# A gated cross-attention and MoE-attention layer: the cross-attention runs two slots sooner, the second normalised x is transposed by VectorE blocks and DRAM

## The chip, the cores and the metric

The kernel runs on one core of one Trainium2 chip. The metric is the device time of one execution in microseconds (us), lower is better. The kernel before took 817.31 us (median of 3 runs, 815.43 to 818.0).

## The reference

The input x has 64 sequences of 128 tokens and 128 channels, and each sequence has a context of 77 rows. Everything is float32.

```python
# cross-attention, gated
xn = layernorm(x)                       # over channels, no scale
keys, values = ctx @ Wk.T, ctx @ Wv.T ; queries = xn @ Wq.T
x  = x + tanh(g_xattn) * softmax(queries @ keys.T / sqrt(128)) @ values
# mixture-of-experts attention, gated
h  = layernorm(x)                       # 16 experts
logits = normalise(h) @ normalise_columns(sim_matrix) - sigmoid(gates)
w  = softmax over the experts with logits > 0 (the two largest if there is none) of relu(logits)
q, k, v = sum_e w[:, e] * (h @ q_proj[e]), the same with k_proj, v_proj
o  = softmax(q @ k.T / sqrt(128)) @ v   # within a sequence
x  = x + tanh(g_ffn) * sum_e w[:, e] * (o @ o_proj[e])
```

## The kernel before, in words

The 64 sequences are worked in 16 groups of 4 (`G = 4`, `NG = 16`), so that a tile has 512 token columns. Each engine has its instruction stream written out by hand in the same frame: `passes(body)` calls `body(i)` for i = 0 to 17, and a body runs over 16 slots `s`, one for each expert. In pass i, TensorE accumulates q, k and v of group i (line 1292: in each slot 9 matmuls of 128x512 in fp16, for high and low halves of weights and of scaled tokens), and between the experts it does work of other groups: the cross-attention of group g1 = i + 2, the second layer norm and the gate of g2 = i + 1, the attention and the output experts of gc = i - 1, and the end of the output experts of gd = i - 2. The output experts are 8 pairs a group (`y_pair`, two times three matmuls each, line 1321), one in every second slot.

Nothing but the semaphores orders the engines against each other. Each engine takes its own stream in order, so a wait on one instruction holds everything behind it on that engine. SyncE (its DMA queue is SPq in the rows) issues nearly all DMAs, and also waits in order.

Steps that the change touches, in the kernel before, with slot numbers:

- Cross-attention of g1: `ctxT_out` (ScalarE, slot 6), `kx_product` (TensorE, 7), `kxT_out` (ScalarE, 7), the scores (`small_product`, four parts within expert 9, line 1385), `x_max` (VectorE, 9, line 1125), `x_exps` and `vx_out` (ScalarE, 10, lines 784 and 792), `vx_product` (TensorE, 10, line 1431), the 32x32 block transpose of px (VectorE, 11), its way through DRAM (SyncE, 12: `px_rows` out, wait, `px_mix` in), `pxT_out` (ScalarE, 12, line 806), `att_product` (TensorE, 14, line 1445), `x1_add` (VectorE, 14, line 1136), `second_stats` (VectorE, 15, lines 923 and 927).
- Second norm of g2, in the following pass: `second_rstd` (GpSimd, 0, lines 594 to 599), `second_norm` (GpSimd, 1), `x2_norm` (ScalarE, 1, line 725), `x2_transpose` (TensorE, 2, line 1401: four 128x128 transposes into bank m0), `x2T_out` (ScalarE, 2, line 733), then the gate logits (`small_product` in expert 4, line 1377), `gate_logits`, `gate_mask`, `gate_softmax` (VectorE, 4, 5 and 6), and `weight_rows` with three `spread_q` broadcasts of 512 KB (SyncE, 9).
- `x2T_p` then holds the transposed tokens, and `zq_scale` (VectorE, line 1063), `zq_high` (ScalarE, 690) and `zq_low` (GpSimd, 611) make each expert's scaled tokens `LEAD = 4` slots ahead of their matmuls.
- In slot 15 ScalarE empties the q, k and v banks (line 845); TensorE's next pass waits for that.
- In slot 7 TensorE makes oT of gc, ScalarE copies its high half and VectorE makes the low half (`oT_low`, line 1078); the third matmul of the first `y_pair` in slot 8 waits for the low half.

v, the first normalised x (from group 3 on) and the attention weights pc already take a way through DRAM in place of a TensorE transpose: VectorE transposes 32x32 blocks (line 994), `blocks_out` writes 256 KB to `blk_rows` (line 428), and `blocks_in` reads it back with four DMAs of 64 KB in block order (line 434).

Of the kernel before, what the change touches and what calls it, by code (L numbers as in the profile page):

```python
# [13 lines left out]
P = 128  # L14
# [16 lines left out]
X_HEAD = 3  # L31

# [17 lines left out]
def flamingo_gated_moe_attention(nc, x, ctx_in, g_xattn, g_ffn, Wk, Wq, Wv, sim_matrix, gates,  # L50
# [11 lines left out]
    with ExitStack() as ctx:  # L62
# [97 lines left out]
        blk_rows = nc.dram_tensor("blk_rows", [3, 4, 32, N], F32, kind="Internal").ap()  # L160
# [4 lines left out]
        pc_blk = sb("pc_blk", [P, 4, G, 32])  # L165
        w_rows = nc.dram_tensor("w_rows", [NG, E * G, P], F32, kind="Internal").ap()
# [83 lines left out]
        x2T_sb = sem("x2T_sb")  # L250
        x2T_moved = sem("x2T_moved")
# [132 lines left out]

        def before(g, e, slots):
            return (g, e - slots) if e >= slots else (g - 1, E + e - slots)
# [8 lines left out]
        MAX_AT, SHARE_AT = (0, 2), ((0, 4), (0, 6))  # L395
# [4 lines left out]
        def _(sp):  # L400
# [83 lines left out]

            def body(i):
                g1, g2, gc, gd = i + 2, i + 1, i - 1, i - 2
                for s in range(E):
                    if s in (2, 4):
                        spread_q(i, PAIRS - 2 + s // 4)
                    if s == 2 and 0 <= gc < NG - 1:  # L490
                        wait(sp, v_blk_done, gc + 1)
                        wait(sp, v_mix_in, 64 * gc)
                        blocks_out(0, v_blk, v_blk_out)
                    if s == 2 and X_HEAD <= g1 < NG:
                        wait(sp, xn_blk_done, g1 - X_HEAD + 1)
                        wait(sp, xn_mix_in, 64 * (g1 - X_HEAD))
                        blocks_out(1, xn_blk, xn_blk_out)
# [25 lines left out]
                    if s == 11 and has(gd) and gd < NG - 1:  # L523
                        store(gd)
                    if s == 12 and has(g1):
                        n = g1 - P_HEAD
                        wait(sp, px_blk_done, n + 1)
                        wait(sp, px_mix_in, 48 * n)
                        sp.dma_start(px_rows.rearrange("i t r -> (i t) r"),
                                     px_blk[:].rearrange("p j b n -> p (j b n)")).then_inc(px_blk_out, 16)  # L530
                        wait(sp, px_blk_out, 16 * (n + 1))
                        wait(sp, pxT_sb, g1)
                        for j in range(3):
                            keys = min(32, S - 32 * j)
                            sp.dma_start(px_mix[32 * j:32 * j + keys].rearrange("t i b n -> t i (b n)"),
                                         px_rows[:, 0:keys, P * j:P * (j + 1)].rearrange("i t r -> t i r")
                                         ).then_inc(px_mix_in, 16)
# [24 lines left out]
        def _(pool):  # L562
# [102 lines left out]
        def _(act):  # L665
# [55 lines left out]
            def x2_norm(g):  # L721
                wait(act, rstd2_step, 3 * g + 3)
                wait(act, x2T_ps, g)
# [113 lines left out]
            def body(i):  # L837
                g1, g2, gc, gd = i + 2, i + 1, i - 1, i - 2
                for s in range(E):
                    if s == E - 1 and has(i):  # L840
# [6 lines left out]
                    if s == 6 and has(g1):  # L847
                        ctxT_out(g1)
# [13 lines left out]
                    if s == 1 and has(g2):  # L862
                        x2_norm(g2)
                    if s == 2 and has(g2):
# [21 lines left out]
                    if s == 5 and has(g1):  # L886
                        xnT_out(g1)
                    if s == 5 and has(g2):
                        gate_exps(g2)
                    if s == 7 and has(g1):  # L890
# [5 lines left out]
                    if s == 10 and has(g1):  # L896
                        x_exps(g1)
                    if s == 10 and has(g1):
# [3 lines left out]
                    if s == 12 and has(g1):  # L902
# [17 lines left out]
        def _(dve):  # L920
# [257 lines left out]
            def body(i):  # L1178
                g1, g2, gc, gd = i + 2, i + 1, i - 1, i - 2
                for s in range(E):  # L1180
                    for g, e in zq_at(i, s):
                        zq_scale(g, e)
                    if s == 11 and has(g1):
# [33 lines left out]
                    if s == 3 and has(g2):  # L1217
                        x2_norm_inverse(g2)
                    if s == 4 and has(g2):
                        gate_logits(g2)  # L1220
                    if s == 5 and has(g2):
                        gate_mask(g2)
                    if s == 6 and has(g2):
                        gate_softmax(g2)
                    if s == 9 and has(g1):
# [3 lines left out]
                    if s == 11 and has(g1):  # L1229
# [5 lines left out]
                    if s == 14 and has(g1):  # L1235
                        x1_add(g1)
                    if s == 15 and has(g1):
                        second_stats(g1)
                    if (i, s) == MAX_AT:
# [23 lines left out]
        def _(pe):  # L1263
# [108 lines left out]
            def small_product(i, s, b):  # L1372
                g1, g2 = i + 2, i + 1
                if s == 4 and has(g2):
                    if b == 0:
                        wait(pe, x2T_sb, g2 + 1)
                    last = nc.tensor.matmul(m0[:, b * E:(b + 1) * E], x2T[:, tok(b)], sn[:],  # L1377
# [3 lines left out]
                if s == 9 and has(g1):  # L1381
# [67 lines left out]
            def head():  # L1449
# [7 lines left out]
                for b in range(G):  # L1457
                    small_product(-2, 9, b)
# [13 lines left out]
                for b in range(G):  # L1472
                    small_product(-1, 9, b)
# [4 lines left out]
            def body(i):  # L1478
                g1, g2, gc, gd = i + 2, i + 1, i - 1, i - 2
                for s in range(E):  # L1480
# [17 lines left out]
                    if s == 2 and has(g2):  # L1498
# [6 lines left out]
                    if s == 5 and g1 < X_HEAD:  # L1505
# [3 lines left out]
                    if s == 7 and has(g1):  # L1509
# [21 lines left out]
                    if s == 10 and has(g1):  # L1531
                        vx_product(g1)
                    if s == 14 and has(g1):
# [33 lines left out]
```

## Time and profile before

| | |
|---|---|
| median of 3 runs | 817.31 us |
| the profiled execution | 816.46 us |
| its span, first to last instruction | 814.6 us |
| busy: TensorE, VectorE, GpSimd, ScalarE | 96%, 74%, 59%, 53% |
| DMA, mean of 16 engines | 45.7% for the queue of SyncE |
| granted TensorE clock, mean | 1.000 |

The profiled execution is 1.86 us longer than its span; that part lies around the first and the last instruction. The stretches of one pass below are cut at the start of the attention scores (line 1394). In a row of the timeline the first number is when an instruction started, the second how long it took; matmuls overlap, so the distance between two starts says what one costs TensorE, and not its duration. "idle before" is time in which an engine waited, and the name behind the arrow is what ended it.

### The profile page before, as it was taken

Reading aid. Unit: us, or ns where it says so; the run is one execution under the profiler, and the core shown is the slowest. Engines: PE = TensorE matmul, PEld = TensorE weight load, DVE = VectorE, ACT = ScalarE, POOL = GpSimd, SP = SyncE. Lnnn points to the kernel's source line nnn. Section 1 sums busy time; section 2 is a strip of 40 time slices with the busy share of each in tenths; the row PEclk is TensorE's granted clock in tenths of the full one; section 3 lists DMA queues with packets and bytes.
Section 4 is the critical chain, followed back from the end, with each engine's and each line's share of the span. In section 5 each row is a group of like instructions: output and inputs, shape, how many; then the busy total and the mean of one; then the engine's idle time right before and its main releaser. Section 6 shows DMA issues by size and latency. Waiting matters only on the chain.

```text
span 814.6 us, 13947 instructions
## 1 busy us (share of the span) xinstructions
PE 784.9 (96%) x4011; PEld 421.3 (52%) x4011; DVE 602.7 (74%) x2026; ACT 434.5 (53%) x1130; POOL 483.4 (59%) x703
## 2 busy tenths in 40 slices
PE   5589999999999999999999999999999999999998
PEld 4445554555555555555555555555555555544444
DVE  2878686869598686868868686886868687685648
ACT  5555645456464645646464564646456454643435
POOL 3275656565585656567665656766565675655534
PEclk9999999999999999999999999999999999999999
DMA  7464664544544443455444445545444554343200
GB/s 184 123 217 151 187 195 138 179 159 139 170 153 148 144 163 118 139 172 155 147 144 135 145 137 171 158 146 144 150 129 138 169 165 136 112 138 119 64 14 27
DMA packets 89195, 116.50 MB, mean 143 GB/s; under 512 B 13734, under 2 KB 62398, under 8 KB 89118
## 3 DMA queue, kind: packets, MB, share of 16 engines
q1 hardware_dynamic: 88398, 115.52, 45.7%
q8 instruction: 32, 0.52, 0.2%
q14 instruction: 45, 0.37, 0.1%
q10 hardware_dynamic: 720, 0.08, 0.1%
HBM read 94.27 MB, written 21.30 MB: 142 GB/s over the span
## 4 chain that ended last, share of the span: by engine, by line
PE 71%; DVE 15%; DMA 5%; issue 3%; POOL 2%; ACT 2%; SPq 2%; DVEq 0%; ACTq 0%; POOLq 0%
PE acc_q L1292 15%; PE acc_k L1292 15%; PE acc_v L1292 15%; PE oT_p L1321 8%; PE y L1321 8%; DVE x_all L1093 3%; DVE zq_full L1063 3%; PE m L1394 2%; PE m L1445 1%; DVE logit L1008 1%; DMA px_rows<-px_blk 1%; PE m L1431 1%; PE m L1385 1%; PE m L1377 1%; DMA stage<-in_L_ffn_k_proj_dram 1%
## 5 line engine op out<-in xcount | busy, mean ns | idle before, releaser
L611 POOL TENSOR_TENSOR zq<-zq_full,zq 128x512 f16<-128x512 f32 x256 | 297.9, 1171 | 278.0 <-ACT zq L690 277.1
L690 ACT ACTIVATE zq<-zq_full 128x512 f16<-128x512 f32 x256 | 159.7, 633 | 219.6 <-DVE zq_full L1063 219.2
L1292 PE MATMUL acc_q<-zq,w_hi 128*128 128x512 f16 x510 | 193.3, 379 | 0.0
L1292 PE MATMUL acc_k<-zq,w_hi 128*128 128x512 f16 x510 | 193.3, 379 | 0.0
L1292 PE MATMUL acc_v<-zq,w_hi 128*128 128x512 f16 x510 | 193.2, 379 | 0.0
L1063 DVE TENSOR_TENSOR zq_full<-wq_bc,x2T_p 128x512 f32<-128x512 f32 x256 | 167.6, 668 | 2.7 <-DMA wq_bc<-w_rows 2.3
L1093 DVE SCALAR_TENSOR_TENSOR x_all<-y,w_out,x_all 128x128 f32<-128x128 f32 x356 | 121.9, 342 | 60.1 <-issue 40.7
L1093 DVE SCALAR_TENSOR_TENSOR x_all<-oT_p,w_out,x_all 128x128 f32<-128x128 f32 x356 | 121.4, 341 | 0.1
L626 POOL TENSOR_TENSOR x_all<-stage,x_all 128x128 f32<-128x128 f32 x240 | 100.4, 456 | 19.9 <-DVE x_all L1093 13.4
L1292 PE MATMUL acc_q<-zq,w_lo 128*128 128x512 f16 x255 | 96.7, 379 | 0.0
L1292 PE MATMUL acc_v<-zq,w_lo 128*128 128x512 f16 x255 | 96.6, 379 | 0.0
L1292 PE MATMUL acc_k<-zq,w_lo 128*128 128x512 f16 x255 | 96.6, 379 | 0.0
L1321 PE MATMUL y<-w_hi,oT 128*128 128x512 f16 x236 | 89.6, 380 | 1.8 <-ACT stage L717 0.9
L1321 PE MATMUL oT_p<-w_hi,oT 128*128 128x512 f16 x236 | 89.5, 379 | 0.0
L1292 PEld LDWEIGHTS acc_v<-zq,w_hi 128*128 128x128 f16 x510 | 53.6, 105 | 53.3
L1292 PEld LDWEIGHTS acc_q<-zq,w_hi 128*128 128x128 f16 x510 | 51.8, 102 | 51.4 <-POOL zq L611 0.6
L1292 PEld LDWEIGHTS acc_k<-zq,w_hi 128*128 128x128 f16 x510 | 49.8, 98 | 53.3
L1136 DVE SCALAR_TENSOR_TENSOR x_all<-m,rsum_x,x_all 128x128 f32<-128x128 f32 x64 | 18.0, 344 | 74.2 <-PE m L1445 74.2
L717 ACT ACTIVATE stage<-oT_p,w_out 128x128 f32<-128x128 f32 x116 | 32.6, 361 | 30.6 <-issue 19.2
L1321 PE MATMUL oT_p<-w_lo,oT 128*128 128x512 f16 x118 | 44.7, 379 | 0.0
L1321 PE MATMUL y<-w_lo,oT 128*128 128x512 f16 x118 | 44.7, 379 | 0.0
L1292 PEld LDWEIGHTS acc_k<-zq,w_lo 128*128 128x128 f16 x255 | 26.8, 105 | 26.7
(223 smaller groups left out, 1108.3 us busy)
## 6 DMA issues: line engine op xcount, KB each, us to landing
wq_bc<-w_rows SPq DMA_DIRECT2D x128, 512.0 KB, 4.3
blk_rows<-v_blk SPq DMA_DIRECT2D x15, 256.0 KB, 4.2
v_mix<-blk_rows SPq DMA_DIRECT2D x60, 64.0 KB, 2.0
blk_rows<-pc_blk SPq DMA_DIRECT2D x15, 256.0 KB, 3.2
pcT<-blk_rows SPq DMA_DIRECT2D x60, 64.0 KB, 2.0
out_dram<-x_all SPq DMA_DIRECT2D x15, 256.0 KB, 4.0
blk_rows<-xn_blk SPq DMA_DIRECT2D x13, 256.0 KB, 2.6
xn_mix<-blk_rows SPq DMA_DIRECT2D x52, 64.0 KB, 3.4
```

Source lines behind the costliest of these rows:

```text
L611: nc.gpsimd.tensor_tensor(zq[:, 1, e % Z_SLOTS, :], zq_full[:, e % F_SLOTS, :], zq[:, 0, e % Z_SLOTS, :], ALU.subtract).then_inc(zq_lo_poo ...
L626: nc.gpsimd.tensor_tensor(total, y_sc[:, n // 2 % 2, b, j, :], total, ALU.add).then_inc(y_pool_added, 1)
L690: nc.scalar.activation(zq[:, 0, e % Z_SLOTS, :], zq_full[:, e % F_SLOTS, :], ACT.Copy).then_inc(zq_hi_done, 1)
L717: last = nc.scalar.activation(dst, bank[:, tok(j)], ACT.Copy, scale=w_out[:, g % 2, e, b0 + b:b0 + b + 1])
L1008: link(nc.vector.tensor_tensor(logit[:], logit[:], sig[:].unsqueeze(1).broadcast_to([P, G, E]), ALU.subtract), 1)
L1063: nc.vector.tensor_tensor(zq_full[:, e % F_SLOTS, :], wq_bc[:, e // 2 % W_SLOTS, e % 2], x2T_p[:], ALU.mult).then_inc(zq_full_done, 1)
L1093: nc.vector.scalar_tensor_tensor(out=rows(x_all, g, b0 + b), in0=bank[:, tok(j)], scalar=w_out[:, g % 2, e, b0 + b:b0 + b + 1], in1=rows(x ...
L1136: last = nc.vector.scalar_tensor_tensor(out=rows(x_all, g, b), in0=m1[:, tok(b)], scalar=rsum_x[:, b:b + 1], in1=rows(x_all, g, b), op0=AL ...
L1292: last = nc.tensor.matmul(acc[m][:], w[:, m, s, :], zq[:, half, s % Z_SLOTS, :], start=(s == 0 and n == 0), stop=(s == E - 1 and n == 2))
L1321: last = nc.tensor.matmul(bank[:], oT[:, g % 2, half, tok(b)], w[:, O, QUAD * k:QUAD * (k + 1), :].rearrange("p e c -> p (e c)"), start=(n ...
L1377: last = nc.tensor.matmul(m0[:, b * E:(b + 1) * E], x2T[:, tok(b)], sn[:], start=True, stop=True)
L1394: done = nc.tensor.matmul(m1[:, tok(b)], qT[:, tok(b)], kT[:, tok(b)], start=True, stop=True)
```

## The change

Cross-attention of g1 moves two slots forward in every pass but pass 0 (`sooner(i)` is 2 there, and 0 in pass 0), and `second_stats`, `second_rstd`, `second_norm` and `x2_norm` of g1 now come in the same pass, in slots 13, 13, 15 and 15. From group 3 on (`X2_HEAD = 3`) the second normalised x takes the way through DRAM in place of `x2_transpose`. In pass 0 the gate steps move one slot back (`late(i)` is 1 there), the second part of the share of the largest output weight moves from slot 6 to slot 7, `xn_transpose` and `xnT_out` from 5 to 6, and px goes out in slot 11, ahead of a broadcast. SyncE's order changes: `weight_rows` in slot 8, px out and in interleaved with the broadcasts in slots 9 and 10, first normalised x back in slot 3, and the new transfers in slots 0 and 1.

```diff
+        blk_rows = nc.dram_tensor("blk_rows", [4, 4, 32, N], F32, kind="Internal").ap()
+        x2_blk = sb("x2_blk", [P, 4, G, 32])
+        x2_mix = sb("x2_mix", [P, 4, G, 32])
...
+        def sooner(i):
+            return 0 if i == 0 else 2
+        def late(i):
+            return 1 if i == 0 else 0
-        MAX_AT, SHARE_AT = (0, 2), ((0, 4), (0, 6))
+        MAX_AT, SHARE_AT = (0, 2), ((0, 4), (0, 7))
...
 # SyncE, body
-                    if s in (2, 4):
-                        spread_q(i, PAIRS - 2 + s // 4)
-                    if s == 2 and 0 <= gc < NG - 1:
+                    if s == 0 and X2_HEAD <= g2 < NG:
+                        wait(sp, x2_blk_done, g2 - X2_HEAD + 1)
+                        wait(sp, x2_mix_in, 64 * (g2 - X2_HEAD))
+                        blocks_out(3, x2_blk, x2_blk_out)
+                    if s == 0 and 0 <= gc < NG - 1:
                         wait(sp, v_blk_done, gc + 1)
                         wait(sp, v_mix_in, 64 * gc)
                         blocks_out(0, v_blk, v_blk_out)
+                    if s == 1 and X2_HEAD <= g2 < NG:
+                        wait(sp, x2_blk_out, 16 * (g2 - X2_HEAD + 1))
+                        wait(sp, x2T_sb, g2)
+                        blocks_in(3, x2_mix, x2_mix_in)
+                    if s in (2, 4):
+                        spread_q(i, PAIRS - 2 + s // 4)
...
-                    if s == 4 and X_HEAD <= g1 < NG:
+                    if s == 3 and X_HEAD <= g1 < NG:
                         wait(sp, xn_blk_out, 16 * (g1 - X_HEAD + 1))
...
-                    if s == 9 and has(g2):
+                    if s == 8 and has(g2):
                         weight_rows(g2)
-                        for j in range(3):
+                    if s == 9 and has(g1) and i > 0:
+                        px_out(g1)
+                    if s == 9:
+                        spread_q(g2, 0)
+                    if s == 10 and has(g1) and i > 0:
+                        px_in(g1)
+                    if s == 10:
+                        for j in (1, 2):
                             spread_q(g2, j)
+                    if s == 11 and has(gd) and gd < NG - 1:
+                        store(gd)
+                    if s == 11 and i == 0:
+                        px_out(g1)
+                        px_in(g1)
...
 # GpSimd, body
-                    if s == 0 and i > 0 and has(g2):
+                    if s == 0 and i == 1:
                         second_rstd(g2)
+                    if s == 13 and i > 0 and has(g1):
+                        second_rstd(g1)
                     for g, e in zq_at(i, s):
                         zq_low(g, e)
-                    if s == 1 and has(g2):
+                    if s == 1 and i < 2:
                         second_norm(g2)
+                    if s == 15 and i > 0 and has(g1):
+                        second_norm(g1)
...
 # ScalarE
             def x2T_out(g):
-                wait(act, x2T_ps, g + 1)
                 wait(act, x2T_moved, g)
                 wait(act, logit_ps, g)
-                nc.scalar.activation(x2T[:], m0[:], ACT.Copy, scale=X_UP).then_inc(x2T_sb, 1)
+                if g < X2_HEAD:
+                    wait(act, x2T_ps, g + 1)
+                    nc.scalar.activation(x2T[:], m0[:], ACT.Copy, scale=X_UP).then_inc(x2T_sb, 1)
+                else:
+                    wait(act, x2_mix_in, 64 * (g - X2_HEAD + 1))
+                    nc.scalar.activation(x2T[:].rearrange("p (b i n) -> p b i n", b=G, n=32),
+                                         x2_mix[:].rearrange("p i b n -> p b i n"), ACT.Copy,
+                                         scale=X_UP).then_inc(x2T_sb, 1)
...
+                    if s == E - 1 and i > 0 and has(g1):
+                        x2_norm(g1)
                     if s == E - 1 and has(i):
                         wait(act, cscore_ps, i)
...
+                    if s == 3 and i > 1 and has(g2):
+                        x2T_out(g2)
...
 # VectorE, body (px blocks, x_max, x_sum, x1_add: slot - sooner(i); gate: slot + late(i))
+                    if s == 13 and i > 0 and has(g1):
+                        second_stats(g1)
...
+                    if s == 15 and i > 0 and has(g1):
+                        wait(dve, x2_done, g1 + 1)
+                        wait(dve, x2_blk_out, 16 * (g1 - X2_HEAD))
+                        blocks_transposed(x2_blk, x2[:], x2_blk_done)
...
 # TensorE, body (kx_product, scores, vx_product, att_product: slot - sooner(i))
-                    if s == 2 and has(g2):
+                    if s == 2 + late(i) and g2 < X2_HEAD:
                         x2_transpose(g2)
-                    if s == 5 and g1 < X_HEAD:
+                    if s == 6 and g1 < X_HEAD:
                         xn_transpose(g1)
```

## Rows read from the trace of the kernel before

**Rows 1.** The page, busy time by engine: us, share of the span, instructions.
```profile
PE 784.9 (96%) x4011; PEld 421.3 (52%) x4011; DVE 602.7 (74%) x2026; ACT 434.5 (53%) x1130; POOL 483.4 (59%) x703
```

**Rows 2.** Stretches of one pass: us, busy PE, PEld, DVE, ACT, POOL, clock, DMA share, GB/s.
```profile
184.84:232.08 47.24, 47.24 (x249) 25.35 (x248) 36.91 (x127) 26.13 (x69) 29.52 (x43) 1.00 0.48 149
...
326.55:373.99 47.44, 47.38 (x249) 25.36 (x248) 36.74 (x127) 26.07 (x70) 29.96 (x44) 1.00 0.48 149
```

**Rows 3.** TensorE's waits over the span: us in total, times, longest.
```profile
PE m L1401 <- ACT x L725: 3.0, 2, 1.8
...
PE oT_p L1283 <- DVE wmax_d L961: 1.2, 1, 1.2
PE oT_p L1522 <- DMA pcT<-blk_rows: 1.1, 1, 1.1
...
PE y L1321 <- ACT stage L717: 0.9, 1, 0.9
...
PE m L1445 <- ACT pxT L806: 0.8, 1, 0.8
```

**Rows 4.** Timeline of TensorE in one steady pass.
```profile
424.11 0.60 PE L1401 MATMUL m<-ident,x 128*128 128x128 f32 x4
424.55 0.38 PE L1321 MATMUL y<-w_hi,oT 128*128 128x512 f16 x1
...
428.22 0.29 PE L1377 MATMUL m<-sn,x2T 128*128 128x16 f32 x2
...
442.26 0.38 PE L1321 MATMUL y<-w_lo,oT 128*128 128x512 f16 x1
442.70 0.39 PE L1321 MATMUL y<-w_hi,oT 128*128 128x512 f16 x1
...
444.01 0.34 PE L1385 MATMUL m<-kxT,xnT 128*128 128x77 f32 x2
444.19 0.38 PE L1292 MATMUL acc_q<-zq,w_hi 128*128 128x512 f16 x1
...
459.41 1.06 PE L1445 MATMUL m<-vx,pxT 77*128 77x128 f32 x8
460.30 0.38 PE L1321 MATMUL y<-w_hi,oT 128*128 128x512 f16 x1
```

**Rows 5.** Timeline of VectorE, the same pass.
```profile
430.58 1.19 DVE L1008 TENSOR_TENSOR logit<-logit,sig 128x64 f32<-128x64 f32 x1
...
441.95 0.69 DVE L1078 TENSOR_TENSOR oT<-oT_p,oT 128x512 f16<-128x512 f32 x1 [1.18 <-ACT oT L895]
...
446.22 0.48 DVE L1125 TENSOR_REDUCE nmax_x<-m 128x4 f32<-128x308 f32 x1 [0.21 <-PE m L1385]
...
460.50 1.13 DVE L1136 SCALAR_TENSOR_TENSOR x_all<-m,rsum_x,x_all 128x128 f32<-128x128 f32 x4 [5.29 <-PE m L1445]
...
465.10 0.38 DVE L927 BATCH_NORM_AGGREGATE mv<-bn 128x2 f32<-128x6 f32 x4
...
465.97 0.70 DVE L994 STREAM_TRANSPOSE v_blk<-vT 128x512 f32<-128x512 f32 x1
```

**Rows 6.** Timeline of ScalarE, the same pass.
```profile
456.27 0.63 ACT L806 ACTIVATE pxT<-px_mix 77x512 f32<-77x512 f32 x1 [2.19 <-DMA px_mix<-px_rows]
...
462.53 0.60 ACT L845 ACTIVATE qT<-acc_q 128x512 f32<-128x512 f32 x1 [2.56 <-PE acc_q L1292]
...
468.68 1.64 ACT L725 ACTIVATE x<-x_all,shift,rstd 128x128 f32<-128x128 f32 x4
```

**Rows 7.** Timeline of GpSimd, the root for the second norm, first and last step.
```profile
466.30 0.23 POOL L594 TENSOR_SCALAR shift<-mv 128x4 f32<-128x4 f32 x1
...
468.02 0.20 POOL L599 TENSOR_TENSOR shift<-shift,rstd 128x4 f32<-128x4 f32 x1
```

**Rows 8.** Issue to landing, by tile: v_blk (its 15 writes).
```profile
DMA to landing us min/median/max: 4.1/4.2/4.8
```

**Rows 9.** The same for the DRAM tensor blk_rows (mostly its 172 reads).
```profile
DMA to landing us min/median/max: 1.8/2.1/4.8
```

More of the change, by code:

```diff
@@ L483, in head, with px_out, px_in @@
                     spread_q(0, j)
+            def px_out(g):
+                n = g - P_HEAD
+                wait(sp, px_blk_done, n + 1)
+                wait(sp, px_mix_in, 48 * n)
+                sp.dma_start(px_rows.rearrange("i t r -> (i t) r"),
+                             px_blk[:].rearrange("p j b n -> p (j b n)")).then_inc(px_blk_out, 16)
+            def px_in(g):
+                n = g - P_HEAD
+                wait(sp, px_blk_out, 16 * (n + 1))
+                wait(sp, pxT_sb, g)
+                for j in range(3):
+                    keys = min(32, S - 32 * j)
+                    sp.dma_start(px_mix[32 * j:32 * j + keys].rearrange("t i b n -> t i (b n)"),
+                                 px_rows[:, 0:keys, P * j:P * (j + 1)].rearrange("i t r -> t i r")
+                                 ).then_inc(px_mix_in, 16)
             def body(i):
@@ L846, in body @@
                                                  scale=1.0 / (X_UP * W_UP)).then_inc(acc_sb[m], 1)
-                    if s == 6 and has(g1):
+                    if s == 6 - sooner(i) and has(g1):
                         ctxT_out(g1)
@@ L861, in body @@
                                              ACT.Copy).then_inc(v_tok_sb, 1)
-                    if s == 1 and has(g2):
+                    if s == 1 and i < 2:
                         x2_norm(g2)
-                    if s == 2 and has(g2):
+                    if s == 2 + late(i) and i < 2:
                         x2T_out(g2)
@@ L885, in body @@
                                              ACT.Copy).then_inc(cpT_sb, 1)
-                    if s == 5 and has(g1):
+                    if s == 3 and i > 1 and has(g2):
+                        x2T_out(g2)
+                    if s == (5 if i else 6) and has(g1):
                         xnT_out(g1)
-                    if s == 5 and has(g2):
+                    if s == 5 + late(i) and has(g2):
                         gate_exps(g2)
-                    if s == 7 and has(g1):
+                    if s == 7 - sooner(i) and has(g1):
                         kxT_out(g1)
@@ L895, in body @@
                         nc.scalar.activation(oT[:, gc % 2, 0, :], oT_p[:], ACT.Copy).then_inc(oT_hi_done, 1)
-                    if s == 10 and has(g1):
+                    if s == 10 - sooner(i) and has(g1):
                         x_exps(g1)
-                    if s == 10 and has(g1):
                         vx_out(g1)
@@ L901, in body @@
                         x2T_move(g2)
-                    if s == 12 and has(g1):
+                    if s == (11 if i else 12) and has(g1):
                         pxT_out(g1)
@@ L1182, in body @@
                         zq_scale(g, e)
-                    if s == 11 and has(g1):
+                    if s == 11 - sooner(i) and has(g1):
                         wait(dve, xexp_done, g1 + 1)
@@ L1216, in body @@
                         blocks_transposed(pc_blk, pc[:], pc_blk_done)
-                    if s == 3 and has(g2):
+                    if s == 3 + late(i) and has(g2):
                         x2_norm_inverse(g2)
-                    if s == 4 and has(g2):
+                    if s == 4 + late(i) and has(g2):
                         gate_logits(g2)
-                    if s == 5 and has(g2):
+                    if s == 5 + late(i) and has(g2):
                         gate_mask(g2)
-                    if s == 6 and has(g2):
+                    if s == 6 + late(i) and has(g2):
                         gate_softmax(g2)
-                    if s == 9 and has(g1):
+                    if s == 9 - sooner(i) and has(g1):
                         x_max(g1)
@@ L1228, in body @@
                         first_stats(g1 + 1)
-                    if s == 11 and has(g1):
+                    if s == 11 - sooner(i) and has(g1):
                         x_sum(g1)
@@ L1373, in small_product @@
                 g1, g2 = i + 2, i + 1
-                if s == 4 and has(g2):
+                if s == 4 + late(i) and has(g2):
                     if b == 0:
                         wait(pe, x2T_sb, g2 + 1)
+                        wait(pe, vx_sb, g2 + 1)
                     last = nc.tensor.matmul(m0[:, b * E:(b + 1) * E], x2T[:, tok(b)], sn[:],
@@ L1380, in small_product @@
                         last.then_inc(logit_ps, 1)
-                if s == 9 and has(g1):
+                if s == 9 - sooner(i) and has(g1):
                     if b == 0:
@@ L1508, in body @@
                         ctx_transpose(g1)
-                    if s == 7 and has(g1):
+                    if s == 7 - sooner(i) and has(g1):
                         kx_product(g1)
@@ L1530, in body @@
                         y_end_sums()
-                    if s == 10 and has(g1):
+                    if s == 10 - sooner(i) and has(g1):
                         vx_product(g1)
-                    if s == 14 and has(g1):
+                    if s == 14 - sooner(i) and has(g1):
                         att_product(g1)
```

34 lines of the change are left out of this document (12 added, 22 removed).

## The prediction

> **What bounds the kernel now.** I read the busy table first: TensorE is busy 96% of the span, VectorE 74%, the others under 60% [rows 1]. Then I cut the span into passes at the attention scores. In four passes (137 to 327 us) TensorE is busy for the whole 47.24 us; in the eight from 327 to 706 us a pass takes 47.44 us and about 0.06 us of it shows as idle [rows 2]. The granted clock is 1.00 throughout, the upper level of 2.4 GHz, so no clock enters the sum. A steady pass is a full TensorE queue: what leaves that queue is gained one for one, and other engines matter only if they come late. The extra 0.2 us has a place in the timeline: the third matmul of the first output pair starts 0.44 us after the second, not 0.22 (442.26 to 442.70), and VectorE's oT_low runs from 441.95 to 442.64 just before it [rows 4, 5]. VectorE worked from the gate logits until there almost without a gap, and one of its steps, the subtraction of the sigmoid, took 1.19 us [rows 5]. Last, TensorE's waits outside the steady passes: 1.8 us for x2, 1.2 us for the maximum of the output weights and 0.8 us for pxT in pass 0, 1.1 us for pcT and 0.9 us for a staged pair in pass 1 [rows 3].
>
> **The transposes that leave TensorE.** The four transposes take TensorE's queue from 424.11 to 424.55, that is 0.44 us [rows 4]. Groups 3 to 15 lose them: 13 x 0.44 = 5.7 us. Each of them lies in a pass with a full queue, so the whole sum is on the path. One page speaks of another size: the Trainium skill, TensorE: Matmul & The Clock Gate, section Part 4: PE-mode transpose, gives about 275 ns for one 128x128 transpose in a kernel's context; 52 of them would be 14.3 us by that. The recorded durations here are near that figure, but the starts in the full queue are 0.11 us apart, and the sum goes by the starts.
>
> **What comes in their place, and what hides it.** VectorE gets one block transpose a pass, 0.70 us by the one for v [rows 5], on an engine with over 9 us idle in a pass [rows 2]. ScalarE's copy of x2T stays. SyncE gets one write of 256 KB and four reads of 64 KB. None is on TensorE, so each costs nothing while its result is in time. I follow the chain in the clock of the pass shown, before any of the gain is taken off.
>
> The attention product starts at 459.41; two slots sooner means ahead of two experts (18 matmuls at 0.216 us) and one pair (6 more), 5.2 us, so 454.2, done 455.1 [rows 4]. Then: x1_add 0.2 us later, 1.1 us; one zq_scale 0.6; statistics 1.3 (0.9 for the four, 0.4 for the aggregates, of which the row is shown); bn2 is ready near 458.3 [rows 5]. GpSimd's root runs 1.92 us (466.30 to 468.22) [rows 7], and it stands ahead of a low half now: done 460.2. The low halves behind it slide 2 us, but they are made 5 us or more ahead of their matmuls. x2_norm takes 1.64 us [rows 6]: done near 462.0. It stands ahead of the emptying of q, k and v, which begins at 462.53 [rows 6]. Cover 0.5 us, and some 0.5 us more before the next pass's matmuls would stand. After its cover each us is one us a pass.
>
> VectorE's block transpose comes behind the adds of the pair of slot 14. That pair begins on TensorE at 460.30 [rows 4], ends 1.3 us on, and its eight adds take 2.1 us, so the blocks are ready at about 464.6. SyncE issues the write at 464.9; a write of this size lands 4.2 us after issue [rows 8]: 469.1. Four reads are issued in 1.7 us and land 2.1 us after issue by the median [rows 9], near 472.5. ScalarE is busy with the exponentials until about 473.0, so x2T is ready at 473.6. TensorE asks for it in expert 4 of the next pass, 428.22 plus one new period of 46.8: 475.0 [rows 4]. Cover 1.4 us. The operation is not in the trace of before for this tile, so its bounds: with every read at the 1.8 us minimum the answer is the same, since ScalarE is then the later one; with the write at 4.8 us (the slowest of v) and the reads at 4.8 us [rows 8, 9] x2T comes 2.8 us later than I reckon, and TensorE would stand 1.4 us a pass, 18 us in all. I take the median, since the slow ones lie in the first passes beside the input loads. Behind the new wait on SyncE stand v's transfer, two broadcasts, xn and pc. v's blocks are ready only after x2's. The broadcast for experts 12 and 13 is issued 4 us later than before but used in slot 8; xn's reads end near slot 5; pc goes out within 0.4 us of its old time, because its blocks are what it waits for.
>
> **The cross-attention two slots sooner.** Scores and product both move over two experts and a pair, so px keeps its time for the way through DRAM: pxT is done at 456.9 for a product at 459.41 [rows 4, 6], a cover of 2.5 us; because oT's product is no longer between them I reckon 1.8 us. No broadcast stands ahead of px out any more, one stands ahead of px in; I count these against each other. What changes for TensorE is where its own fillers lie: the scores, 4 x 0.18 us (444.01 to 444.19 for one) [rows 4], and the value product (0.87 us) now come between the gate logits and the first output pair. That gives VectorE's gate chain 1.6 us more, and it takes on x_max there, 0.4 us between starts [rows 5], and must wait for the scores. By my count oT_low ends 0.4 us ahead of its matmul, where now it is 0.2 us late. So the 0.2 us goes: 8 passes x 0.2, and 0.3 us in pass 14, 1.9 us. Bounds: 1.9 us gained, or with a second step as slow as the 1.19 us one, 1 us more on VectorE and 0.6 us lost a pass.
>
> That step is a place for a rule. It took 1.19 us in the slow passes for a tile that others of its size take in 0.23, and it ended with GpSimd's low half beside it. The Trainium skill, SBUF — State Buffer, section SBUF: two separate sides, says that VectorE with two SBUF inputs and GpSimd take one port pair in turn, each for a whole instruction. By that rule the root and the low halves that move could block another step of the chain; the row can't tell which, and it stands in the rival below with bounds of its own from rows.
>
> **The first passes.** In pass 0 the transpose comes a slot later, so x2 is there, but TensorE then comes to experts whose low halves GpSimd has only just made; the wait for the maximum goes as well; and px of group 2 may then be later than its product, since its write stands behind three broadcasts. Bounds 0 and 3.8 us, the sum of the three waits [rows 3]; I take 1.5, under the middle, since each of them has a follower. In pass 1 the scores come ahead of oT's product (0.7 us of 1.1 [rows 3]), v is written ahead of a broadcast, and ScalarE no longer waits for pxT ahead of the staged pair: bounds 0 and 2.0 us, I take 2.0, since both mechanisms are direct.
>
> **Sum.** 5.7 + 1.9 + 1.5 + 2.0 = 11.1 us. The profiled execution took 816.46 us, which is 0.85 us under the median of the runs. 816.46 - 11.1 = 805.4, and put against the median 806.2. I predict 806.2 us.
>
> **Rivals.**
> 1. Only the transposes pay. The early waits turn into others (broadcasts, low halves, DMAs beside the loads) and VectorE's chain keeps its 0.2 us: 5.7 us, 817.3 - 5.7 = 811.6. For it: three of the waits end by DMA or by a chain of several engines. Against it: the added 1.6 us on TensorE's side. Chance 0.22.
> 2. VectorE's gate chain gets later, by the lock or by x_max that waits for the scores: it loses 0.6 us a pass over 12 passes, 7 us against 11.1 - 1.9 = 9.2: 2 us gained, 815. Chance 0.06.
> 3. The slower one: the way of x2 through DRAM is longer than its cover. The place is x2T_out in slot 3, the price is each us past 1.4 us, 13 times, and it decides from 0.85 us of standing a pass on (11.1 / 13), a round trip 2.3 us longer than I reckon. With the slow ends above, 1.4 us a pass, it is 18 - 11 = 7 us slower: 824. For it: it is one serial chain from the attention product over five engines and two transfers, and the reads from blk_rows reach 4.8 us. Against: v and xn take the same way each pass, and only pcT in pass 1 was ever late by more than 1 us [rows 3]. Chance 0.10.
> 4. x2_norm holds back the emptying of q, k and v: past 1 us together, each us costs 13; about 0.3 us a pass, 4 us, 810. Chance 0.07. The same chain started sooner or later than I count moves this one first.
>
> The forecast has 0.55. A change under 0.3%, 2.5 us, can't be told from none here; faster is the forecast, rival 1, rival 4 and a part of rival 2: 0.85. Same 0.05, slower 0.10. The forecast's own range is 803.5 to 808.5 (the early waits fully gained, or none of them); with rivals 1 and 4 the range is 803.5 to 813.
>
> **What would show it.** The pass from scores to scores should be 46.80 us with TensorE at 100%; no x2 transposes after 100 us; between the second and the third matmul of the first pair 0.22 us; x2_norm ending before the first emptying; ScalarE's x2T copy with no wait for the DMA of x2_mix, and the first logit matmul with none before it; in passes 0 and 1 less than 2 us of idle TensorE. A period above 46.8 with a wait at line 1377 is rival 3, at an expert's first matmuls rival 4, at the first pair rival 2. I am wrong in the sum if the period is 46.8 and the time above 810.

## The result

The changed kernel takes 805.83 us (median of 4 runs, 805.12 to 806.04) against 817.65 us for the kernel before (4 runs, 815.43 to 818.54): ratio 0.9858, 95% interval 0.9837 to 0.9879. Timed again beside later experiments it took 805.17 us, and the kernel before 816.43 us: 11.3 us less there, 11.8 us less here. The forecast of 806.2 us holds. The profiled executions differ by 10.4 us (816.46 and 806.04 us).

Busy time of the changed kernel, by engine, answers to [rows 1]:

```profile
PE 778.8 (97%) x3959; PEld 416.8 (52%) x3959; DVE 608.7 (76%) x2039; ACT 434.5 (54%) x1130; POOL 483.4 (60%) x703
```

TensorE has 52 instructions fewer, the 13 x 4 transposes, and VectorE 13 more, the blocks. Next, stretches of the changed kernel from the scores of one pass to the next, answering to [rows 2] (us, busy PE, PEld, DVE, ACT, POOL, granted clock, DMA share, GB/s): pass 0 from its first expert, pass 1, one steady pass, pass 14.

```profile
43.74:91.79 48.05, 44.67 (x213) 21.96 (x214) 36.61 (x106) 24.76 (x53) 34.31 (x39) 0.96 0.55 177
91.79:135.12 43.33, 43.33 (x231) 23.68 (x230) 32.95 (x110) 25.62 (x65) 28.17 (x40) 1.00 0.57 182
...
415.73:462.50 46.77, 46.77 (x244) 24.97 (x244) 37.21 (x129) 26.11 (x69) 29.66 (x44) 1.00 0.52 161
...
696.34:740.87 44.53, 44.11 (x218) 21.48 (x218) 31.15 (x103) 19.38 (x48) 26.80 (x34) 1.00 0.42 138
```

The same cuts in the kernel before, to subtract:

```profile
44.48:91.44 46.96, 42.81 (x212) 21.93 (x213) 34.46 (x106) 24.94 (x53) 33.75 (x38) 1.00 0.53 169
91.44:137.59 46.15, 44.09 (x231) 23.50 (x230) 33.34 (x109) 24.55 (x62) 26.28 (x36) 1.00 0.56 172
```

Every steady pass of the changed kernel takes 46.77 us and TensorE is busy for all of it; the eight that took 47.44 us and the four of 47.24 us are alike now. The difference of 10.4 us adds up: 7.3 us in the 12 steady passes, 2.8 in pass 1, 0.4 in pass 14, 0.7 in the head (everything ahead of the first expert, which starts at 43.74 and not 44.48), 0.2 behind pass 14 and around the span, less 1.0 in pass 0. The 0.7 us of the head can't be claimed for the change: in the twelve profiles of the experiments below, none of which edits the head, the first expert starts anywhere from 43.38 to 44.27.

TensorE's waits in the changed kernel (us in total, times, longest), answering to [rows 3]:

```profile
PE m L1505 <- ACT pxT L856: 2.3, 1, 2.3
...
PE m L1461 <- ACT x L769: 1.1, 1, 1.1
```

The 2.3 us are pxT in pass 0; before it was 0.8. The waits for pcT and for the staged pair in pass 1 are gone, of x2's wait in pass 0 nothing is left (the 1.1 us is group 0's, in the head), and the wait for the maximum is gone too. Around the 2.3 us the timeline of TensorE shows a second thing:

```profile
83.12 1.16 PE L1505 MATMUL m<-vx,pxT 77*128 77x128 f32 x8 [2.28 <-ACT pxT L856]
84.11 0.38 PE L1351 MATMUL acc_q<-zq,w_hi 128*128 128x512 f16 x1
84.33 0.38 PE L1351 MATMUL acc_q<-zq,w_lo 128*128 128x512 f16 x1
...
85.54 0.63 PE L1351 MATMUL acc_k<-zq,w_hi 128*128 128x512 f16 x1
85.97 0.63 PE L1351 MATMUL acc_v<-zq,w_hi 128*128 128x512 f16 x1
```

Behind the wait matmuls start 0.43 us apart and not 0.22: the clock fell from 2.4 to 1.2 GHz for some 3.5 us. The granted clock of that stretch, and two matmuls of the first expert of pass 0:

```profile
84.83:88.24 3.41, 3.41 (x10) 1.23 (x9) 3.06 (x14) 1.94 (x4) 1.10 (x1) 0.50 0.71 265
```
```profile
44.12 0.63 PE L1369 MATMUL acc_q<-zq,w_lo 128*128 128x512 f16 x1
44.55 0.63 PE L1367 MATMUL acc_k<-zq,w_hi 128*128 128x512 f16 x1
```

The first matmuls of pass 0 have the same wide spacing, until 47.36 here and until 48.84 in the kernel before, although the mean granted clock reads 1.00 there. In the run with the value product in slot 10 (below) it reads 0.50 from 43.79 to 49.17, with the same spacing. Over all profiles 6 to 13 matmuls are slow there, 0.21 us each, so a single profile can't settle a difference of 1 us in pass 0.

The first output pair of a steady pass, VectorE's oT_low and ScalarE around x2, from the timeline of the changed kernel, answer to [rows 4 to 7]; TensorE, VectorE, ScalarE:

```profile
422.06 0.29 PE L1437 MATMUL m<-sn,x2T 128*128 128x16 f32 x2
...
437.70 0.38 PE L1380 MATMUL y<-w_lo,oT 128*128 128x512 f16 x1
437.91 0.38 PE L1380 MATMUL y<-w_hi,oT 128*128 128x512 f16 x1
```
```profile
424.43 1.19 DVE L1061 TENSOR_TENSOR logit<-logit,sig 128x64 f32<-128x64 f32 x1
...
436.41 0.69 DVE L1131 TENSOR_TENSOR oT<-oT_p,oT 128x512 f16<-128x512 f32 x1 [1.18 <-ACT oT L949]
...
457.55 0.70 DVE L1047 STREAM_TRANSPOSE x_blk<-x 128x512 f32<-128x512 f32 x1
```
```profile
421.11 0.63 ACT L781 ACTIVATE x2T<-x_mix 128x512 f32<-128x512 f32 x1
...
453.89 1.65 ACT L769 ACTIVATE x<-x_all,shift,rstd 128x128 f32<-128x128 f32 x4 [0.40 <-POOL shift L636]
456.14 0.60 ACT L897 ACTIVATE qT<-acc_q 128x512 f32<-128x512 f32 x1 [0.60 <-PE acc_q L1351]
```

The third matmul of the pair comes 0.21 us after the second, and oT_low ended 0.8 us before it, at 437.10. The sigmoid's subtraction still takes 1.19 us. Before, it took that long in exactly the eight passes of 47.44 us and 0.22 us in the four of 47.24; now it is long in 11 of the 12 steady passes and none of them is longer for it. The stall went though the slow step is there. x2_norm ends at 455.54, 0.6 us before q's bank is emptied. x2T ends at 421.74, 0.3 us before the logits take it, with no wait for the DMA before it: the last of the four reads had landed at 417.16, 4.0 us before ScalarE turned to them.

### The profile page after: what moved, and what is told of

Its sections match the earlier page's. It is cut to its first block, busy times and chain, and to the rows that moved or that the text cites. A ratio compares the mean times of both kernels' runs of the same rounds, so it can differ in the third digit from the quotient of the medians.

```text
span 804.2 us, 13947 instructions
## 1 busy us (share of the span) xinstructions
PE 778.8 (97%) x3959; PEld 416.8 (52%) x3959; DVE 608.7 (76%) x2039; ACT 434.5 (54%) x1130; POOL 483.4 (60%) x703
## 4 chain that ended last, share of the span: by engine, by line
PE 88%; DVE 5%; ACT 2%; POOL 2%; DMA 1%; issue 1%; SPq 0%; DVEq 0%; ACTq 0%; POOLq 0%
PE acc_k L1351 19%; PE acc_v L1351 19%; PE acc_q L1351 19%; PE oT_p L1380 9%; PE y L1380 9%; PE m L1505 2%; PE m L1454 2%; PE oT_p L1582 2%; DVE x_all L1146 1%; PE m L1491 1%; PE m L1445 1%; PE m L1437 1%; POOL zq L648 1%; PE m L1485 1%; DVE zq_full L1116 1%
## 5 line engine op out<-in xcount | busy, mean ns | idle before, releaser
L1351 PEld LDWEIGHTS acc_v<-zq,w_lo 128*128 128x128 f16 x255 | 25.0, 98 | 26.8 <-issue 0.3
```

Of the source, the lines that this page charges most:

```text
L1351: last = nc.tensor.matmul(acc[m][:], w[:, m, s, :], zq[:, half, s % Z_SLOTS, :], start=(s == 0 and n == 0), stop=(s == E - 1 and n == 2))
```

## The experiments

All are edits of the changed kernel; "pass" is the time from scores to scores.

**Transposes back on TensorE.**

```diff
-X2_HEAD = 3
+X2_HEAD = 16
-                    if s == 15 and i > 0 and has(g1):   # VectorE, blocks of x2
+                    if s == 15 and i > 0 and X2_HEAD <= g1 < NG:
```

> The changed kernel with the four transposes of x2 back on TensorE in slot 2 for all groups; everything else stays (cross-attention two slots sooner, norm and root in slots 13 to 15, the order of SyncE). Theory: the transposes are worth their starts in a full queue, 0.44 us in each of 13 passes: pass 47.21 us in place of 46.77, time 5.7 us over the changed kernel, about 811.5. Rival (a transpose costs its recorded duration, 0.27 us): 14 us more, 820. Rival (the DRAM way costs TensorE something elsewhere): less than 3 us more.

811.89 us (ratio to before 0.9932, 0.9911 to 0.9952), pass 47.20 us. That is 6.1 us over the changed kernel's 805.83, and 0.43 to 0.44 us a pass, all of it at the place of the transposes: the starts in the queue are what a transpose costs here, not its recorded duration. The 0.2 us of [rows 4] did not come back with the transposes, so it belongs to the other part of the change. Between these 47.20 us and the 47.24 us of before 0.03 to 0.04 us a pass are left, which were not followed up.

**The order behind x2_norm.** In the first of three, ScalarE empties q, k and v and then makes x2.

```diff
-                    if s == E - 1 and i > 0 and has(g1):
-                        x2_norm(g1)
                     if s == E - 1 and has(i):
                         ...
+                    if s == E - 1 and i > 0 and has(g1):
+                        x2_norm(g1)
```

> x2_norm in slot 15 stands behind the emptying of q, k and v. Its result then comes about 3.5 us later (it starts 1.8 us after the emptying would end it now). Theory from the changed kernel's trace: the blocks of x2 land over 3 us before ScalarE turns to them, so a delay of 2 to 3.5 us through VectorE and DRAM costs at most some tenths a pass; time 806 to 809. Rival (my prediction's count, a cover of 1.4 us): 1 to 2 us of standing at line 1437's matmul in each of 13 passes, 819 to 832.

816.94 us (ratio to before 0.9997): all of the gain gone again. The pass takes 47.65 us, and TensorE waits at the logits in all 13 passes, 0.6 us by the record and 0.88 us from start to start, which is the whole difference. (A record of a wait begins at the modelled end of the matmul before, 0.38 us behind its start, where in a full queue the next starts after 0.22 us; so it leaves out at least 0.16 us.) My theory of some tenths failed. The rival had the place, line 1437, but 1 to 2 us was too much, and its cause, the transfer, is not what the trace shows. VectorE, ScalarE and SyncE's DMA issues of that kernel, one turn of the pass:

```profile
464.25 0.71 DVE L1047 STREAM_TRANSPOSE x_blk<-x 128x512 f32<-128x512 f32 x1 [1.89 <-ACT x L769]
465.46 0.69 DVE L1047 STREAM_TRANSPOSE v_blk<-vT 128x512 f32<-128x512 f32 x1
```
```profile
473.15 0.63 ACT L731 ACTIVATE zq<-zq_full 128x512 f16<-128x512 f32 x1
473.67 0.63 ACT L781 ACTIVATE x2T<-x_mix 128x512 f32<-128x512 f32 x1
```
```profile
467.15 1.74 SPq L449 DMA_DIRECT2D x_mix<-blk_rows  x4
```

The reads of x2 were issued by 468.89 and the last landed at 470.45. ScalarE turned to x2T at 473.67, with no wait for a DMA, straight behind pc's exponentials and a high half. VectorE had stood 1.89 us for x2 with scaled tokens, v's blocks and the maxima behind it, and those maxima are what pc's exponentials wait for.

**VectorE's blocks later as well.** The same, and the blocks of x2 are transposed in slot 1 of the next pass.

```diff
-                    if s == 15 and i > 0 and has(g1):   # VectorE
...
+                    if s == 1 and i > 1 and has(g2):
                         wait(dve, x2_done, g2 + 1)
                         wait(dve, x2_blk_out, 16 * (g2 - X2_HEAD))
                         blocks_transposed(x2_blk, x2[:], x2_blk_done)
```

> As the run with x2_norm behind the emptying, and VectorE's block transpose of x2 moved behind v's blocks, to slot 1 of the next pass, so that VectorE no longer stands 1.9 us for x2 with scaled tokens, v's blocks and the maxima behind it. x2 goes out as late as in that run. Theory: it was VectorE's queue and not the transfer that cost 0.88 us a pass; the pass is 46.8 to 47.1 us again, time 806 to 810. Rival: the transfer's delay cost it, and the pass stays at 47.6 us or above, 817.

812.50 us, pass 47.33 us: 4.4 us better than the run above, although x2 went out as late. So a part of the 0.88 us was VectorE's wait. It missed the 46.8 to 47.1 us: 0.57 us is left, TensorE still waits 0.3 us for x2T, and ScalarE still takes x2T straight behind the exponentials and a high half (at 424.56, with the last read landed at 421.55). One step on VectorE, the scaling of the maxima, accounts for it. That step and GpSimd beside it in this kernel, then the step in the run above:

```profile
420.10 1.05 DVE L1267 TENSOR_SCALAR nmax_c<-nmax_c,score_scale 128x4 f32<-128x4 f32 x1
```
```profile
418.84 2.27 POOL L648 TENSOR_TENSOR zq<-zq_full,zq 128x512 f16<-128x512 f32 x2
```
```profile
470.02 0.23 DVE L1263 TENSOR_SCALAR nmax_c<-nmax_c,score_scale 128x4 f32<-128x4 f32 x1
```

It took 1.05 us here and 0.31 us in the changed kernel, 0.74 us more, and x2T starts 6.28 us behind the scores here and 5.55 us there, 0.73 us later. The step ends within 0.05 us of GpSimd's low halves beside it; in the run above it started at 470.02, when GpSimd's low halves had ended at 469.91, and took 0.23 us. That the low halves hold it up is what these three rows suggest; no run moved them. The later transfer by itself ended no wait of ScalarE.

**x2 read back late.** SyncE issues the four reads of x2 in slot 2, behind v's.

```diff
-                    if s == 1 and X2_HEAD <= g2 < NG:
+                    if s == 2 and X2_HEAD <= g2 < NG:   # and moved behind blocks_in(0, v_mix, ...)
                         wait(sp, x2_blk_out, 16 * (g2 - X2_HEAD + 1))
```

> SyncE issues the four reads of x2 behind v's reads, in slot 2, some 4 us later. Theory: they land near the time at which ScalarE turns to x2T or 1 to 2 us after it; past that cover each us is one us a pass: 0.5 to 2 us in 13 passes, 812 to 832, with TensorE's wait at the gate logits. Rival (the cover is larger, or TensorE has other slack): no change, 806.

823.90 us (ratio 1.0074, 1.0054 to 1.0095), slower than before the change. The last read lands 5.5 us later against the scores than in the changed kernel. ScalarE now does wait for the transfer, and TensorE for ScalarE; ScalarE's row, then TensorE's in all:

```profile
ACT x2T L781 <- DMA x_mix<-blk_rows: 17.1, 12, 2.3
```
```profile
PE m L1437 <- ACT x2T L781: 13.3, 12, 1.9
```

This is the slower rival of the prediction made on purpose: place and sign are as it said, 1.2 to 2.2 us a pass. The order of four DMA issues decides between 12 us gained and 7 lost.

**GpSimd's root behind the low half.**

```diff
-                    if s == 13 and i > 0 and has(g1):
-                        second_rstd(g1)
                     for g, e in zq_at(i, s):
                         zq_low(g, e)
+                    if s == 13 and i > 0 and has(g1):
+                        second_rstd(g1)
```

> GpSimd makes the low half of slot 13 first and then the root of the second norm. Theory: the root ends 2 us later, x2_norm ends 2 us later and holds back the emptying of q, k and v, which has some 1 us of cover in all: TensorE stands 0.8 to 1.2 us at the first expert of 13 passes, 10 to 16 us more, 816 to 822. Rival: the order of the two on GpSimd is worth nothing, 806.

823.45 us. TensorE's waits and ScalarE's timeline of that kernel:

```profile
PE acc_q L1351 <- ACT qT L897: 15.5, 13, 1.2
```
```profile
466.13 1.65 ACT L769 ACTIVATE x<-x_all,shift,rstd 128x128 f32<-128x128 f32 x4 [2.75 <-POOL shift L636]
467.68 0.57 ACT L897 ACTIVATE qT<-acc_q 128x512 f32<-128x512 f32 x1
```

x2_norm waits 2.75 us for the root (0.40 in the changed kernel), and q's bank is emptied behind it: 1.2 us by the record and 1.36 us from start to start in each of 13 passes, 17.6 us in all, a little above the expected range. The root came 2.35 us later and 1.36 us of it reached TensorE, so the cover is 1.0 us. One place of one instruction group on an engine that is busy 60% of the time is worth more than the whole change's gain.

**The cover of oT_low.** The first leaves the value product in slot 10, the second gives VectorE three more maxima.

```diff
-                    if s == 10 - sooner(i) and has(g1):   # TensorE; ScalarE's vx_out too
+                    if s == 10 and has(g1):
                         vx_product(g1)
```

> The value product and its copy back in slot 10; the rest as changed. In the changed kernel oT_low ends 0.87 us before the third matmul of the first pair starts, and the value product (0.87 us) lies just ahead of that pair. Theory: the pair then starts 0.87 us sooner and the matmul waits 0 to 0.1 us: pass 46.8 to 46.9 us, time 806 to 807.5, the distance between its second and third matmul 0.22 to 0.3 us. Rival (the scores ahead of the pair matter, the value product does not): exactly as changed, with 0.2 us or more of cover left.

806.56 us, pass 46.90 us. The third matmul starts 0.34 us after the second (436.49 to 436.83). So without the value product in front of the pair 0.13 us a pass comes back of the 0.2 us stall: the scores alone cover a part of it, the scores and this product together all of it, with 0.8 us to spare.

```diff
+                for n in range(3 if g >= 3 else 0):
+                    nc.vector.tensor_reduce(spare_max[:, 3 * g + n], m1[...], AX_X, ALU.max, negate=True)
                 nc.vector.tensor_reduce(nmax_x[:], m1[...], AX_X, ALU.max, negate=True)
```

> VectorE takes the maximum of the cross scores four times in place of once from group 3 on (three of them into a spare tile): 3 x 0.39 = 1.17 us more in its chain ahead of oT_low. Theory: the cover there is 0.87 us, so the third matmul of the first pair is 0.3 us late in 12 passes: pass 47.07 us, time about 3.6 us over the changed kernel, 809.5. Rival (VectorE waits for ScalarE there, so it has slack of its own): no change.

814.22 us, pass 47.50 us: 0.73 us a pass and not 0.3. TensorE of that kernel:

```profile
441.56 0.39 PE L1384 MATMUL y<-w_hi,oT 128*128 128x512 f16 x1 [0.25 <-ACT oT L950]
441.79 0.38 PE L1384 MATMUL y<-w_lo,oT 128*128 128x512 f16 x1
442.29 0.39 PE L1384 MATMUL y<-w_hi,oT 128*128 128x512 f16 x1
```

It stands twice, 0.4 us for the high half and 0.29 us for the low half. The 1.17 us of maxima became 1.5 us, since rs_d behind them took 0.52 us in place of 0.22; 1.5 less the cover of 0.8 us is the 0.7 us measured. That the high half is late too shows the way of the delay. VectorE's record has 1.18 us of waiting for ScalarE just before oT_low, in this run as in the changed kernel, and it is no slack: ScalarE's copy of oT stands behind a high half of scaled tokens that itself waits for VectorE, 0.69 us in the changed kernel and 2.15 us here.

```profile
440.39 0.63 ACT L732 ACTIVATE zq<-zq_full 128x512 f16<-128x512 f32 x1 [2.15 <-DVE zq_full L1117]
440.93 0.58 ACT L950 ACTIVATE oT<-oT_p 128x512 f16<-128x512 f32 x1
```

**Pass 0 as before.** `late` 0 in pass 0, the second share in slot 6, xn's transpose in slot 5.

```diff
-            return 1 if i == 0 else 0
+            return 0
-        MAX_AT, SHARE_AT = (0, 2), ((0, 4), (0, 7))
+        MAX_AT, SHARE_AT = (0, 2), ((0, 4), (0, 6))
...
-                    if s == 6 and g1 < X_HEAD:   # TensorE; ScalarE's xnT_out too
+                    if s == 5 and g1 < X_HEAD:
                         xn_transpose(g1)
```

> Pass 0 has its gate steps, its transpose of xn and the second part of the share of the largest output weight where they stood before; px's place ahead of a broadcast stays. Theory: the change's shifts in pass 0 gained nothing, since TensorE then waits longer for px (2.3 us against 0.8) and its clock falls: undone, pass 0 is 0 to 1.5 us shorter, time 804.5 to 806. Rival (my prediction): undone, 1.5 us longer, 807.5.

805.79 us, the same as the changed kernel. In its profile TensorE again waits for x2 and for the maximum, and no longer for px; the scores of pass 1 start at 89.18. The shifts in pass 0 moved the waits to px and gained nothing that can be measured.

**px ahead of two broadcasts in pass 0**, then also **pc's write ahead of xn's reads in pass 1**, then also **the output weights' high half in slot 10**.

```diff
-                    if s == 10:
+                    if s == 10 and i > 0:
                         for j in (1, 2):
                             spread_q(g2, j)
...
                         px_out(g1)
                         px_in(g1)
+                        for j in (1, 2):
+                            spread_q(g2, j)
```

> In pass 0 two of the three broadcasts of 512 KB are issued behind px instead of ahead of it. Theory: px's write took 4.9 us because it stood behind them; it lands 2 us sooner, TensorE's wait of 2.3 us in pass 0 falls under 1 us and its clock stays at 2.4 GHz there (1.9 us more): 2 to 4 us less, 802 to 804. Rival: the broadcasts are then late for experts 2 to 5 and hold VectorE, no gain or 1 us lost.

803.87 us. The write of px was issued at 74.92 and its read at 76.80, 1.9 us later; in the changed kernel 74.83 and 79.78, 4.9 us. TensorE's wait for px is gone, but it comes to oT's product in pass 1 2.0 us before pcT (0.5 us in the changed kernel where its clock did not fall), so a good part of the gain is given back there.

```diff
+                    if s == 3 and i == 1:   # ahead of blocks_in(1, xn_mix, ...)
+                        wait(sp, pc_blk_done, gc + 1)
+                        wait(sp, cpT_in, 64 * gc)
+                        blocks_out(2, pc_blk, pc_blk_out)
...
-                    if s == 4 and 0 <= gc < NG - 1:
+                    if s == 4 and 1 <= gc < NG - 1:
                         wait(sp, pc_blk_done, gc + 1)
```

> px ahead of two broadcasts in pass 0, and in pass 1 the write of pc issued ahead of the reads of xn. Theory: with px ahead, TensorE came to oT's product in pass 1 2.0 us before pcT; the write goes out 1.2 us sooner, so that wait falls to about 1 us: 1 us under the run with px ahead, 802.5 to 803.5. Rival: xn's reads are then late for the cross scores and the wait moves there, no gain.

803.22 us (802.26 to 803.68); no wait for pcT is left (oT's product starts at 102.53, 105.16 in the run above). On the same chip the changed kernel took 805.17 us (804.58 to 807.04), so the two moves together are worth 2.0 us.

```diff
-        HIGH_AT = (0, 9)
+        HIGH_AT = (0, 10)
```

> The same, and the high half of the output weights made on ScalarE in slot 10 of pass 0, behind the exponentials. Theory: with px ahead of the broadcasts TensorE no longer waits for px, so this gains nothing: within 0.5 us of the run before it. Rival: pass 0 is still bound by ScalarE there, 1 to 2 us less.

802.44 us, ratio to before 0.9831 (0.9818 to 0.9845), the fastest version. It is 0.8 us faster than the run before it by the medians, which is not clear of the spread of the runs; the two profiled executions took 802.43 and 802.26 us, and oT's product starts no earlier (102.69). A gain of this edit is not shown.

**The changed kernel again.**

> The changed kernel once more, on the same chip as the two versions with px ahead, to compare with: 805 to 806.5. Theory: its clock falls for some us in pass 0 only when TensorE has waited 2 us for px, so pass 0's length varies by up to 2 us between executions while the steady pass stays at 46.77 us. Rival: the fall of the clock has nothing to do with that wait and is found elsewhere.

805.17 us. In this profile TensorE waited 1.7 us for px, the clock did not fall behind that wait, and the scores of pass 1 started at 89.44 and not 91.63. Of the nine profiles with px behind the broadcasts and the new pass 0, four have slow matmuls within 2 us of the wait's end: those with 2.3 to 2.4 us of wait (the changed kernel, the late read of x2, the root behind the low half) and one with 1.7 us (the blocks later). The five without them waited 1.4 to 1.8 us, so the length of the wait alone does not tell whether they come. My expectation that the clock falls in pass 0 only there was wrong too: in every profile, that of the kernel before included, the first matmuls of pass 0 are slow; the rows of 44.12 and 44.55 above are two of them.

## Why the prediction was right

**The full queue.** 13 x 0.44 = 5.7 us was predicted; putting the transposes back cost 0.43 to 0.44 us a pass, and the period is 46.77 us where 46.80 was named.

**The 0.2 us of the first pair.** Gone in all eight passes, as reckoned; in pass 14 the wait stays (0.3 us), because no cross-attention is left there to stand between. 1.6 us and not 1.9. I reckoned 0.4 us of cover, it is 0.8.

**The chain behind the attention product.** x2_norm ends 0.6 us before the emptying, with 0.5 predicted, and the cover up to TensorE is 1.0 us by the run that moved the root behind one low half, as predicted. Past it that run lost 1.36 us a pass. That was rival 4, to which I gave 0.07: it did not happen, but only the edge that comes next was nearer.

**The cover of x2T.** 1.4 us was predicted and 0.3 us measured. The step that was wrong is ScalarE's time for x2T: it starts 0.95 us before the logits and not 2.0 us (473.0 against 475.0 in the prediction). The count left out the high half of scaled tokens that stands between the exponentials and x2T, 0.52 us from start to start, and had the exponentials end 0.5 us too early against the logits. The transfer was mis-sized the other way: x2's write landed 2.0 us after its issue by the median (2.5 at most) where I took v's 4.2, so the data lie ready 4.0 us before ScalarE takes them and not 0.5. The price I set on a slow DMA was too high, and the one on VectorE's and ScalarE's order too low. The forecast of no wait held with less than a quarter of the cover it named.

**The first passes.** 3.5 us in sum was predicted. The profile of the result shows 1.8: 2.8 gained in pass 1 and 1.0 lost in pass 0. The profile in which the clock did not fall behind the wait for px shows 3.0: 1.3 gained in pass 0 (45.57 us from first expert to scores, 46.85 before) and 1.7 in pass 1, where TensorE then stands for pcT. "No clock enters the sum" was thus wrong for pass 0, whose first matmuls are at the lower clock in both kernels. Pass 1 gave more than its recorded idle of 2.0 us, because a record leaves out at least 0.16 us of each wait. In pass 0 the sentence on px behind three broadcasts came true in full, the sign "less than 2 us of idle TensorE" did not (3.4 us, 2.3 of them for px), and the experiment without the shifts shows that the 1.5 us I booked there are worth nothing by themselves.

Sum: 11.1 us predicted; 11.8 us between the medians (11.3 when timed again), 10.4 us between the profiled executions. In these the transposes gave 5.7 us as predicted, the first pair 1.6 where I had 1.9, the first passes 1.8 where I had 3.5. The sum had no term for 0.7 us in the head, 0.4 in the steady passes and 0.2 behind them. So the mechanism that carries half of the gain is shown, and that the total came this close is in part luck: a miss of 2.0 us was met by 1.3 us that I did not forecast.

## What to carry to other kernels

Where the bounding engine's queue is full, price what leaves it by the distance between starts in the trace, and then look only for who comes late. When a result moves to a way through DRAM, follow the in-order queues that wait for it, not only the transfer: here a wait of 1.9 us on VectorE, with other engines' inputs queued behind it, cost more than the DMA. Idle time in front of an instruction is no slack when what ends it waits in turn for the same engine. Small writes that a chain waits for go ahead of what is less urgent on the same queue; doing so at two places gave 2.0 us more.

## What was not expected of the hardware

A wait of 2.28 us of TensorE in pass 0 was followed by 3.4 us at 1.2 GHz (start to start 0.43 us in place of 0.22), and the scores of pass 1 came 2.2 us later than in the execution without it; about 1 us of that came back in pass 1, where TensorE otherwise waits for pcT. And a 192 KB write landed 4.9 us after its issue with three broadcasts of 512 KB in flight (4.3 us in the second profile of the same kernel, 4.5 in the kernel before), 2.7 us with two (pass 0 as before) and 1.9 us with one (px ahead). With two or three it landed 0.5 us behind the last of them each time.
